# Adding a residual inside the down product's bank with an identity matmul, and copying the sum out on ScalarE

## The reference, cut to what matters

```python
def _L1_ffn_ref(x, norm_w, router_w, w1, w2, sg, su, sd):
    residual = x
    h = _rmsnorm(x, norm_w)
    flat = h.reshape(-1, H)
    ...
    routed = jnp.sum(y.reshape(T, K, H) * topk_w[..., None].astype(ys.dtype), axis=1)
    shared = jax.nn.silu(flat @ sg) * (flat @ su) @ sd
    out = residual + (routed + shared).reshape(B, S, H)
    return out
x = x + _L0_ffn_ref(_L0_cond_ref(x, side, side, L0_cond_w, L0_cond_u, cond_512), ...)
x = x + _L1_ffn_ref(_L1_cond_ref(x, side, side, L1_cond_w, L1_cond_u, cond_512), ...)
```

## Time and profile before

| | |
|---|---|
| median of three runs | 4693.35 us (4689.81 to 4693.54) |
| the profiled execution's own time | 4695.12 us |
| its span, first to last instruction | 4693.4 us |
| TensorE matmul busy, weight load busy | 95%, 76% |
| VectorE busy, ScalarE busy | 55%, 38% |
| mean granted TensorE clock | 0.978 |

### The profile page before, as it was taken

How to read it: one execution, slowest core, us unless ns; L and a number is a source line. 1 busy time by engine, 2 the same in 40 slices (tenths; PEclk the granted TensorE clock), 3 DMA queues, 4 the chain that set the end, 5 groups by cost and what they waited for, 6 DMA issues and landing times.

```text
span 4693.4 us, 60863 instructions
## 1 busy us (share of the span) xinstructions
PE 4473.3 (95%) x19860; PEld 3545.8 (76%) x19863; DVE 2569.9 (55%) x2765; ACT 1795.0 (38%) x2596; POOL 703.4 (15%) x934
## 2 busy tenths in 40 slices
PE   6677999999999999999999999999999999999998
PEld 2245877777777777878888887887888878888787
DVE  8999999999999653433333434444341243333432
ACT  5665555555555332222222323334231242222321
POOL 1000000000000017111111111111111111111111
PEclk8888999999999999999999999999999999999999
DMA  6664866767676766654344545555452264444532
GB/s 227 248 255 177 292 237 249 261 225 272 246 264 232 263 219 185 242 180 114 99 127 112 165 116 161 169 163 188 141 170 58 59 202 128 112 112 116 161 108 62
DMA packets 247927, 835.08 MB, mean 178 GB/s; under 512 B 28160, under 2 KB 61056, under 8 KB 222976
## 3 DMA queue, kind: packets, MB, share of 16 engines
q1 hardware_dynamic: 172944, 572.77, 34.0%
q0 software_dynamic: 47728, 160.07, 15.4%
q10 hardware_dynamic: 27136, 100.67, 5.6%
HBM read 652.40 MB, written 181.01 MB: 178 GB/s over the span
## 4 chain that ended last, share of the span: by engine, by line
PE 85%; DVE 8%; issue 3%; ACT 3%; DMA 1%; DVEq 0%; ACTq 0%; POOL 0%; SPq 0%; POOLq 0%
PE ps L1545 35%; PE ps L1409 24%; PE ps L1559 17%; PE ps L1478 3%; PE ps L1431 1%; PE ps L1534 1%; DVE work L925 1%; DVE work L931 1%; PE ps L1419 1%; PE ps L1429 1%; DMA out<-work 1%; DVE work L952 1%; DVE work L954 1%; DVE work L935 1%; DVE work L958 1%
## 5 line engine op out<-in xcount | busy, mean ns | idle before, releaser
L1545 PE MATMUL ps<-halves 128*128 128x512 f32 x7152 | 1700.8, 394 | 25.8 <-DVE halves L1304 22.3
L1545 PEld LDWEIGHTS ps<-halves 128*128 128x128 f32 x7152 | 1340.0, 189 | 303.7 <-DVE halves L1304 24.4
L1409 PE MATMUL ps<-halves 128*128 128x512 f32 x6144 | 1451.5, 396 | 12.3 <-issue 12.3
L1409 PEld LDWEIGHTS ps<-halves 128*128 128x128 f32 x6144 | 1155.3, 189 | 285.7 <-issue 47.4
L1559 PE MATMUL ps<-halves 128*128 128x512 f32 x3576 | 834.9, 389 | 1.3 <-DVE halves L1324 1.3
L1559 PEld LDWEIGHTS ps<-halves 128*128 128x128 f32 x3576 | 671.2, 188 | 140.8 <-DVE halves L1324 1.6
L1308 DVE TENSOR_TENSOR halves<-ps,halves 128x1024 fp32r<-128x1024 f32 x150 | 183.6, 1224 | 884.4 <-ACT halves L807 884.4
L1304 DVE TENSOR_TENSOR halves<-work,halves 128x1024 fp32r<-128x1024 f32 (+1 forms) x320 | 440.5, 1433 | 114.9 <-ACT halves L811 114.9
L807 ACT ACTIVATE halves<-ps 128x1024 fp32r<-128x1024 f32 x150 | 154.0, 1027 | 849.6 <-PE ps L1545 849.6
L811 ACT ACTIVATE halves<-work 128x1024 fp32r<-128x1024 f32 (+1 forms) x320 | 369.7, 1221 | 96.3 <-PE ps L1559 66.5
L1324 DVE TENSOR_TENSOR halves<-ps,halves 128x256 fp32r<-128x256 f32 x298 | 112.3, 418 | 494.8 <-ACT halves L839 494.8
(11 more groups left out here) (186 smaller groups left out, 3787.8 us busy)
## 6 DMA issues: line engine op xcount, KB each, us to landing
halves<-split_dram SPq DMA_DIRECT2D x512, 512.0 KB, 5.6
work<-expert_w SPq DMA_DIRECT2D x192, 1024.0 KB, 5.7
split_dram<-halves ACTq DMA_DIRECT2D x32, 1024.0 KB, 4.9
plain<-shared_w SPq DMA_DIRECT2D x32, 512.0 KB, 3.2
gated_dram<-work ACTq DMA_DIRECT2D x32, 512.0 KB, 4.2
work<-side_t ACTq DMA_DIRECT2D x32, 512.0 KB, 5.5
work<-x_t ACTq DMA_DIRECT2D x32, 512.0 KB, 3.3
ratio_dram<-work ACTq DMA_DIRECT2D x32, 512.0 KB, 5.0
```

Source lines behind the costliest of these rows:

```text
L1409: last = pe.matmul(bank(k % 4), w, op[:, part], start=(c == 0 and w is w_hi and op is hi), stop=(c == CB - 1 and w is w_lo))
L1545: last = pe.matmul(ps_h[:, a * 512:a * 512 + 512], xp[:, xk * P:(xk + 1) * P], wp[:, rhs], start=(xk == 0 and xp is xhi and wp is whi[q]), ...
```

## The change

Each down product's bank gets its residual from TensorE: ahead of the 24 matmuls stands one with `ident` as weights and `RES[o]` as the moving operand, both plain f32, which opens the accumulation. `down` moves from VectorE's program to ScalarE's, at the same step, as a copy of the bank to `OV`, counted on a semaphore of its own (`down_out`). The waits for bank readers are counted anew (`bank_freed`). VectorE keeps the wait for the product ahead of overwriting `RES[o]`. In ScalarE's fill the copy stands ahead of `out_copy`, squares and sigmoids; in its tail it stands ahead of `out_copy` and of `split_x`.

```diff
+        def bank_freed(h, k, first):
+
+            if first:
+                return "read_out", k - 3
+            at = k - 4 + CB
+            if at < 0:
+                return "read_out", h * READS + (at + 1)
+            downs = list(range(CB)) if final(h, HALVES) else [at_d for at_d in STEP_D]
+            if at in downs:
+                return "down_out", copied(h - 1, downs.index(at))
+            return "read_out", h * READS + (at + 1 - len([d for d in downs if d <= at]))
...
@@ SP, tail
-                sp.wait_ge(s["read_out"], HALVES * STEPS)
+                sp.wait_ge(s["read_out"], HALVES * READS)
+                sp.wait_ge(s["down_out"], HALVES * CB)
...
@@ ScalarE
+            def down(h, o, k, hk):
+                sc.wait_ge(s["product"], hk * STEPS + (k + 1))
+                if o == 0:
+                    sc.wait_ge(s["a_lo_s"], (h + 1) * CB)
+                sc.wait_ge(s["o_tr"], h * CB + (o + 1))
+                sc.activation(OV, bank(k % 4), ACT.Copy).then_inc(s["down_out"], 1)
...
+                    for o in range(CB):
+                        if prev and i == step_d(o) + 1:
+                            down(h - 1, o, number(step_d(o), False), h)
                     for o in range(CB):
                         if prev and i == copy_step(o):
                             out_copy(h - 1, o)
...
                     split_part_hi(0, o // 2, parts(o // 2)[o % 2])
+                    down(HALVES - 1, o, o - CB, HALVES)
                     if o:
                         out_copy(HALVES - 1, o - 1)
...
@@ VectorE
-            def down(h, o, k, hk):
-
-                await_product(hk, k)
-                if o == 0:
-                    ve.wait_ge(s["a_lo_s"], (h + 1) * CB)
-                ve.wait_ge(s["o_tr"], h * CB + (o + 1))
-                ve.wait_ge(s["res"], h * CB + (o + 1))
-                ve.tensor_tensor(OV, bank(k % 4), RES[:, o * HALF:(o + 1) * HALF], ALU.add).then_inc(s["read_out"], 1)
...
-                        if prev and i == step_d(o) + 1:
-                            down(h - 1, o, number(step_d(o), False), h)
...
                             if prev:
-                                ve.wait_ge(s["read_out"], summed(h - 1, o))
+                                await_product(h, number(step_d(o), False))
...
-                    down(HALVES - 1, o, o - CB, HALVES)
...
@@ TensorE
-                wait(pe, "read_out", h * STEPS + (k - 3))
+                wait(pe, *bank_freed(h, k, first))
+                if res:
+                    block, count = res
+                    pe.wait_ge(s["res"], count)
+                    pe.matmul(bank(k % 4), ident[:, :], RES[:, block * HALF:(block + 1) * HALF], start=True, stop=False)
...
-                                             start=(c == 0 and w is w_hi and op is hi), stop=(c == CB - 1 and w is w_lo))
+                                             start=(not res and c == 0 and w is w_hi and op is hi), stop=(c == CB - 1 and w is w_lo))
...
-                pe.wait_ge(s["read_out"], summed(h, o))
+                pe.wait_ge(s["down_out"], copied(h, o))
```

More of the change, by code:

```diff
@@ L206, in adaln_moe @@
             "wv_done num num_w newton1 newton2 sig_steps sig_x gated gated_raw ratio ratio_out gated_out "
-            "split_hi split_lo split_pe chunk product read_out c_hi c_lo sig1_steps sig1 c1 z sq z_hi z_lo res "
+            "split_hi split_lo split_pe chunk product read_out down_out c_hi c_lo sig1_steps sig1 c1 z sq z_hi z_lo res "
             "z_tr logits sums z_copy z_out mean r_ln r_exp newton_r r_set l_copy l_tr l_acc silu_steps silu_sig "
@@ L264, in products, with x_added, copied @@
             return [(i, number(i, first)) for i in range(STEPS) if not (first and i in D_AT)]
[L267 to L271, removed]
-        def scaled_gate(h, j):
-            return h * STEPS + (CB + 2 * j + 1)
+        READS = STEPS - CB
+        def x_added(h, o):
+            return h * READS + (o + 1)
+        def copied(h, o):
+            return h * CB + (o + 1)
+        def scaled_gate(h, j):
+            return h * READS + (CB + 2 * j + 1)
+        def bank_freed(h, k, first):
[8 more added lines that the diff above has]
+            return "read_out", h * READS + (at + 1 - len([d for d in downs if d <= at]))
         PREP = 2 + 3 * BATCH
@@ L710, in silu @@
                 sc.wait_ge(s["product"], h * STEPS + (k + 1))
-                wait(sc, "read_out", h * STEPS + k)
+                wait(sc, "read_out", h * READS + k)
                 sigmoid(SG, bank(k % 4), "silu_steps", h * CB + j, "silu_sig")
@@ L742, in fill @@
                         if i == step_l(o) + 1:
-                            sc.wait_ge(s["read_out"], x_added(h, o, first))
+                            sc.wait_ge(s["read_out"], x_added(h, o))
                             wait(sc, "c1", h * CB + o)
@@ L1393, in _, with product @@
             pe.wait_ge(s["split_lo"], 2 * UNITS_PER_HALF * 4 + 2)
-            def product(h, k, hi, lo, ready, at):
-                wait(pe, "read_out", h * STEPS + (k - 3))
+            def product(h, k, hi, lo, ready, at, first=False, res=None):
+                wait(pe, *bank_freed(h, k, first))
[3 more added lines that the diff above has]
+                    pe.matmul(bank(k % 4), ident[:, :], RES[:, block * HALF:(block + 1) * HALF], start=True, stop=False)
                 for j in range(2):
@@ L1485, in half @@
                         if i >= 2 * CB:
-                            product(h, ks[i], zhi, zlo, "z_lo" if i == 2 * CB else None, h * CB)
+                            product(h, ks[i], zhi, zlo, "z_lo" if i == 2 * CB else None, h * CB, first)
                         elif i in L_AT:
-                            product(h, ks[i], chi, clo, "c_lo" if i == 0 else None, h * CB)
+                            product(h, ks[i], chi, clo, "c_lo" if i == 0 else None, h * CB, first)
                         else:
-                            product(h, ks[i], ahi_s, alo_s, "a_lo_s" if D_AT[i] == 0 else None, (h - 1) * CB)
+                            product(h, ks[i], ahi_s, alo_s, "a_lo_s" if D_AT[i] == 0 else None, (h - 1) * CB,
+                                    res=(D_AT[i], (h - 1) * CB + (D_AT[i] + 1)))
                     for o in range(CB):
@@ L1523, in _ @@
                     transpose_x(0)
-                product(HALVES, o - CB, ahi_s, alo_s, "a_lo_s" if o == 0 else None, (HALVES - 1) * CB)
+                product(HALVES, o - CB, ahi_s, alo_s, "a_lo_s" if o == 0 else None, (HALVES - 1) * CB,
+                        res=(o, (HALVES - 1) * CB + (o + 1)))
                 if o:
@@ L1593, in close @@
                 second_product(g, EXPERTS - 1)
-            pe.wait_ge(s["read_out"], HALVES * STEPS)
+            pe.wait_ge(s["read_out"], HALVES * READS)
+            pe.wait_ge(s["down_out"], HALVES * CB)
             pe.wait_ge(s["o_copy"], HALVES * CB + 1)
```

## The result

The changed kernel takes 4735.77 us, median of three runs (4732.63 to 4741.18), against 4693.35: a ratio of 1.0095, 95% interval 1.0081 to 1.0108. It is slower by 42 us; 46 were forecast. The profiled execution has a span of 4734.1 us, 40.7 more than before.

What follows compares the result with a forecast made beforehand. TensorE was taken to bound the kernel. Halves 1 to 7 (42.1) plus the tail (6.9), less 0.7 at the tail's end and 2.4 for the clock, gave 45.9 us more: 4739 us, range 4727 to 4753.

Steps and rivals of the forecast that it cites:

- The chain of half 3: Waits stay on TensorE, leaving only behind step 14's product through the output store; a 3.67 us gap is the only cover.
- The signs: Expected in the changed profile: 0.86 us pairs, halves 2 to 5 each 6 us longer, gap 0.6 to 0.9 us narrower.
- The added matmul: Identity matmul ahead of each down product: 0.86 us a pair, priced from L1419, bounds 0.24 and 1.10.
- Seven of eight on the path: Halves 1 to 7: seven additions cost 0.86 us each, step 15's hides in TensorE's gap; 6.0 us a half, 42.1 together.
- ScalarE in time by 0.1 us: Step 14: ScalarE's copy ends at 6.2 us, TensorE's product at 6.33, so nothing was added.
- The rival of the late ScalarE: Step 14's margin fails or copies wait behind unit work, so TensorE waits: 52 to 58 us, 4745 to 4751; chance 0.18.
- The tail's -0.7: Tail's end: experts start between 1.4 us sooner and 0.2 us later, depending on the store's landing; -0.7 us taken.
- The clock: Narrower gaps ahead of `by_token` end the slow matmuls in halves 6 and 7, -2.4 us; halves 2 to 5 keep theirs.
- The stores: Output store on the chain behind step 14 in half 3: 5.53 us to land; no change in landing time was priced.
- VectorE's relief at nothing: 64 adds of 0.680 us leave VectorE, 5.4 us a half, priced at nothing.
- VectorE as pace-maker: Rival: VectorE's 5.4 us a half is on the path in halves 1 to 5; -9 us, 4684; chance 0.02.
- the cheap identity: Rival: the identity matmul costs a product matmul's 0.24 us; sum 11 us, 4704; chance 0.03.

Runs made afterwards that it cites:

- the move alone: The changed kernel without the identity matmul, residual left out of the output, against the kernel before: 4687.4 us against 4691.36, ratio 0.9994 (0.9985 to 1.0003).

## Why the prediction was right, and where it was off

**The chain of half 3: read too narrowly.** I had the chain leave TensorE at one place and called that gap the only cover. The profile before has a second place in halves 1 to 4, with 2.66 to 2.81 us idle (and 1.45 more in half 2). It lies behind all the added matmuls and hid none of them, so the count of seven of eight stands; but its clock falls were missing from the sum.

**The signs: half of them.** Halves 2 to 5 should each have been 6 us longer; they were 6.9, 2.8, 3.1 and 2.9. The gap should have been 0.6 to 0.9 us narrower; only half 4's is within a few hundredths of that. The pair's 0.86 us, the chain through the store and the 13 us of `by_token` in halves 6 and 7 came as said.

**The added matmul: right.** 0.86 us from the neighbour L1419 is what L1416 measured, to the hundredth, and nothing waits in front of it. Down the columns of the table it costs 45 to 47 us; I had 49.0 ahead of what it sets free.

**Seven of eight on the path: right.** The chain leaves TensorE behind step 14 as I read it, and the matmul of step 15 ran inside the gap.

**ScalarE in time by 0.1 us: right.** In the changed kernel no half shows a wait of the transposes of step 14, in the run without the matmul it is 0.77 us. The rival of the late ScalarE fell with it.

**The tail's -0.7: right, by luck of the bounds.** From the end of the last product to the experts it was 5.05 us, before 5.74 (both on the chain). The store of block 6 landed in 2.52 us and was what the last copy waited for.

**The clock: right in kind, mis-sized.** I took the falls of halves 6 and 7 as gone, -2.4 us, and kept those of halves 2 to 5, since their gaps stayed as wide as one that had fallen. Measured are no fall in halves 3 to 7, a new one in half 1 and one still in half 2: of the -8.8 us of the last column some 6.6 are the clock, and the second gap gave back 3.4 more. Two steps failed. I held the gaps of halves 2 to 5 at 2.5 us or more, and with the shorter stores they were 1.85, 1.51, 2.84 and 2.24. And I read the gap's width as what decides. Half 4 kept the full clock behind 2.84 us, half 2 lost it behind 1.85. The run without the matmul says the same: half 1 kept it behind 2.43 us, half 4 lost it behind 2.17. Over halves 1 to 7 of all twelve profiles, 48 gaps ahead of `by_token` were under 1.8 us wide and none had a slow matmul behind it; of 30 between 1.85 and 2.95 us, 16 had; all six of 2.98 us or more had. So a narrower gap makes the fall rarer, and in the middle the width alone does not tell for one half. The Trainium skill (TensorE: Matmul & The Clock Gate, Part 1) says that the chip's look at TensorE runs free of the program, so that the same kernel shows different numbers of slow matmuls. No kernel here was traced twice, so no run shows that; gaps of one width that went both ways would fit it. By its rule on gaps (same page, HAM oscillation) neither half 1 nor half 2 of the changed kernel should have fallen; both did, and the measurement decides.

**The stores: missing.** I kept 5.53 us for the store of step 14; it took 3.1 us less over halves 2 to 7. With two identity matmuls it was 4.1 to 4.3 us in every half. Each half of the change alone also shortened these stores, the move by 4.0 us over halves 2 to 7 and the matmul by 2.5. Which other transfers a store meets was not looked into, and that the shifted start is the reason is argued, not shown.

**VectorE's relief at nothing: wrong by 2.2 us, and for a reason worth more.** The add of block 7 delays the third scaling by 0.3 us a half; I had said that TensorE had two blocks to work on, which holds only while these run at the low clock. Larger is what the last two rows of the table show: the relief was covered by the store, not worthless. Uncovered it is roughly 12 to 14 us, part of it VectorE's wait for the transposes that goes with the add, and part of it the clock.

So 49.0 - 0.7 - 2.4 = 45.9 (49.0 being the 42.1 and 6.9 of halves and tail) became 49.0 - 0.7 - 8.8 - 3.1 in this pair of profiles, with half 0 and the second gap on top: 35.5 us where the edit is, against 45.9 forecast. The totals lie nearer together, 41 us in the profiles and 42 in the medians. In the profiles that is luck: 5.2 us of the 41 come from stages without the edit. The rivals on VectorE as pace-maker and on the cheap identity are refuted by the move alone and by the 0.86.

## What to carry to other kernels

Moving an add from a vector engine into a TensorE bank costs TensorE a matmul of its own per bank, 0.86 us here, and with plain f32 operands nearly four times what an fp32r matmul of the same size takes (0.23 us): where TensorE is the bound, price it from the nearest f32 matmul in the trace and count how many lie on the path. Before calling an engine's relief worthless, ask which other wait covers it: here an output store sat ahead of the root in ScalarE's queue, and with the root first the same relief was worth roughly 12 us. Follow the chain through a whole period and list every place where the engine that sets the pace stands still, not only the nearest to the edit. Work placed in a gap of TensorE can make a kernel faster if it keeps the clock up.

## What the runs showed of the hardware that I had not expected

Eight matmuls whose result is thrown away, 1.8 us in each of seven halves, took 6 us off the kernel (ratio 0.9988, 0.9979 to 0.9997), since the f32 routing products behind the gap ran at 1.04 us a pair (half 3; the first pair took 1.92 us in the kernel before). And the 64 output stores of the kernel before, 256 KB each, took between 2.3 and 9.7 us to land, median 5.6; what decides it was not looked into.
